# A graph network kernel on one core: GpSimd clears a scratch tile between gathers, and payload and row slots are handed over by single units

## What is computed

```python
# src, dst: (50000,) node numbers; dst is sorted
h = relu(layernorm(x))
x = x + mlp(h + segment_sum(relu(h[src] + edge_attr_16 @ We + be), dst))      # layer 0
h = relu(layernorm(x))
x = x + ten_steps_of_weighted_sums(h, edge_weight, src, dst)                   # layer 1
h = relu(layernorm(x))                                                         # layer 2, three sublayers:
hx = h @ W_node[l]; ef = relu(edge_attr_3 @ W_e1[l] + b_e1[l]) @ W_e2[l] + b_e2[l]
a = sigmoid(relu(concat(hx[dst], hx[src], edge_attr_3) @ Wa1[l] + ba1[l]) @ Wa2[l] + ba2[l])
h = maybe_relu(layernorm(segment_sum(a * (hx[src] + ef), dst) + bias[l])) + h
h = relu(layernorm(x))
x = x + segment_sum(silu(bn(concat(h[src], h[dst] - h[src]) @ W.T)), src)      # layer 3
```

## Time and profile before

| | |
|---|---|
| three timed runs | 4567.13, 4567.83, 4573.78 us |
| profiled execution, first to last instruction | 5635.3 us (its only time that is given) |
| busy in it: PE, DVE, ACT, POOL | 3433.8, 2812.2, 928.0, 3082.6 us |
| mean granted TensorE clock in it | 0.781 |
| gathers (L770) | 2080, 2085.0 us busy |

### The profile page before, as it was taken

The page is one execution under the profiler, slowest core; times in us unless marked ns, Lnnn a source line. Parts: engine busy times, 40 slices in busy tenths (PEclk is TensorE's granted clock), DMA queues, the critical chain, the costliest instruction groups (busy, mean ns, idle before and its releaser), DMA issues.

```text
span 5635.3 us, 80038 instructions
## 1 busy us (share of the span) xinstructions
PE 3433.8 (61%) x20001; PEld 2425.2 (43%) x20012; DVE 2812.2 (50%) x10008; ACT 928.0 (16%) x3266; POOL 3082.6 (55%) x3058
## 2 busy tenths in 40 slices
PE   2440078878889999656656556666566666344444
PEld 2330034444433444355556455555455556233333
DVE  7840088878621111355555455555555556533333
ACT  0000023333200000011112111112111112111111
POOL 3787676656688880145555345555255554355544
PEclk9999999989899999777777577777677777555555
DMA  4311123323599999411111211112111112011101
GB/s 139 82 26 9 47 67 74 83 70 80 133 331 344 356 352 356 165 40 43 42 43 42 38 41 43 42 43 41 38 43 43 42 43 40 18 20 19 19 18 21
DMA packets 293594, 498.20 MB, mean 88 GB/s; under 512 B 169174, under 2 KB 207203, under 8 KB 291962
## 3 DMA queue, kind: packets, MB, share of 16 engines
q1 hardware_dynamic: 118407, 339.94, 17.0%
q0 software_dynamic: 92160, 115.72, 11.2%
q10 hardware_dynamic: 82800, 40.01, 2.5%
HBM read 435.57 MB, written 58.97 MB: 88 GB/s over the span
## 4 chain that ended last, share of the span: by engine, by line
PE 38%; another core or an unknown queue 21%; DVE 14%; issue 13%; POOL 8%; ACT 2%; DMA 1%; DVEq 1%; ACTq 1%; SPq 0%; POOLq 0%
PE ps L1502 34%; POOL rows_dst L755 8%; DVE arena L1103 3%; DVE arena L1102 2%; PE ps L1728 2%; DVE arena L1121 1%; DVE arena L1119 1%; PE ps L1605 1%; DVE arena L1117 1%; DMA arena<-in_edge_attr_dram 1%; PE ps L1680 1%; DVE arena L1275 1%; ACT arena L1468 1%; DVE arena L1280 1%
## 5 line engine op out<-in xcount | busy, mean ns | idle before, releaser
L770 POOL DMA_INDIRECT arena<-table,arena x2080 | 2085.0, 1002 | 2200.4 <-DMA arena<-rows_dst 1299.9
L1502 PE MATMUL ps<-arena 128*128 128x96 f32 (+3 forms) x9176 | 1605.9, 354 | 573.3 <-issue 174.3
L1502 PEld LDWEIGHTS ps<-arena 128*128 128x128 f32 (+3 forms) x9176 | 1138.9, 207 | 953.3 <-issue 623.6
L1605 PE MATMUL ps<-ident,arena 128*96 128x128 f32 x416 | 149.9, 360 | 1123.1 <-ACT arena L1468 570.6
L1102 DVE TENSOR_SCALAR arena<-iota_row_b,arena 128x128 bf16<-128x128 bf16 x1664 | 438.3, 264 | 695.4 <-remote 518.6
L1502 PE MATMUL ps<-arena,nodes 125*64 125x500 f32 (+2 forms) x3144 | 649.6, 538 | 27.2 <-DVEq L1194 16.5
L755 POOL DMA_INDIRECT rows_dst<-stage,arena x400 | 483.7, 1209 | 196.3 <-issue 121.6
L1103 DVE TENSOR_SCALAR arena<-iota_row_b,arena 128x128 f32<-128x128 bf16 x2080 | 582.5, 298 | 0.0
L1605 PEld LDWEIGHTS ps<-ident,arena 128*96 128x96 f32 x416 | 65.3, 157 | 1190.5 <-ACT arena L1468 588.3
L1115 DVE TENSOR_TENSOR arena<-ps,arena 128x256 f32<-128x256 f32 x416 | 175.4, 422 | 787.3 <-remote 614.9
L728 POOL DMA_INDIRECT rows_src<-stage,stage_at x400 | 485.1, 1213 | 118.5 <-issue 116.6
(11 more groups left out here) (284 smaller groups left out, 3858.7 us busy)
## 6 DMA issues: line engine op xcount, KB each, us to landing
arena<-dense SPq DMA_DIRECT2D x240, 750.0 KB
nodes<-dense SPq DMA_DIRECT2D x60, 750.0 KB
dense<-arena ACTq DMA_DIRECT2D x150, 250.0 KB
arena<-table,arena POOLq DMA_INDIRECT x2080
arena<-dense SPq DMA_DIRECT2D x60, 500.0 KB
arena<-rows_dst SPq DMA_DIRECT2D x208, 96.0 KB
arena<-dense SPq DMA_DIRECT2D x6, 2000.0 KB
arena<-pair_rows SPq DMA_DIRECT2D x12, 976.6 KB
```

What stands on the lines that cost most here:

```text
L770: nc.gpsimd.indirect_dma_start(rows[:, u, k, 0:width], None, frm, bass.IndirectOffsetOnAxis(ap=p[:, c, j, c_other:c_other + 1].bitcast(I32 ...
L1502: return nc.tensor.matmul(to, lhsT, rhs, start=start, stop=stop, skip_group_check=True)
L1605: nc.tensor.transpose(to, pay[:, c, j:j + K, :].rearrange("p k c -> p (k c)"), ident[:]).then_inc(tr_ready, 1)
```

## The change

`CH` goes from 4 to 8, so `UC` is 1: every payload DMA carries one unit (48 KB instead of 96 KB for `pay`, 8 KB instead of 16 KB for `pay2`; 520 such DMAs instead of 260), and the waits for `pay_in` and `slots_free` stand ahead of four gathers instead of eight. TensorE and VectorE wait for `pay_in` at each unit instead of each second one. The carved arrays keep their total size. After each gather GpSimd waits until all scratch clears before this one are complete, and then clears `rest`, 100 float32 in each of 128 partitions; 2080 clears in all. `rest` is read by nobody.

```diff
-CH = 4
+CH = 8
 UC = U // CH
 CT = K * UC
...
+        rest = sb("rest", [128, 100])
...
+        rested = sem("rested")
...
                                     bass.IndirectOffsetOnAxis(ap=p[:, c, j, c_other:c_other + 1].bitcast(I32), axis=0)).then_inc(gathered[u], 16)
 
+                                hold(pool, rested, m * BODY + (u * K + k + 1))
+                                nc.gpsimd.memset(rest[:], 0.0).then_inc(rested, 1)
+
+            pool.sem_inc(rested, 1)
             pool.wait_ge(filled, 16 * 8)
             scatter_dst()
```

## The result

The changed kernel takes 4707.15 us (median of four runs), the kernel before 4567.68 us in the same session. The ratio is 1.0301, with a 95% interval of 1.0288 to 1.0313: slower by 3.0%, 139 us. Forecast were 4699 us and slower.

What follows compares the result with a forecast made beforehand. GpSimd's issue of gathers was taken to bound passes 1 to 4. The clears' 116 us there plus 15 us in pass 0 gave 131 us on 4567.83: 4699 us, 2.9% more, range 4575 to 4860 us.

Steps and rivals of the forecast that it cites:

- The stops belong to the profiled execution: Passes 1 to 4: GpSimd's idle gaps of 4.98 and 10.2 us occur only in the profiled execution, not timed runs.
- GpSimd's issue of gathers bounds passes 1 to 4: Passes 1 to 4, timed: GpSimd needs 5.00 us for a unit's four gathers, the compute side about 4.4.
- The clear, 0.07 us a gather, 116 us: Passes 1 to 4: a clear behind each of 1664 gathers adds 0.07 us, 116 us; ends 0 and 300 us.
- The first reading: Between two gathers: clear 0.18 us plus 0.18 us behind it, 0.36 us for 0.30, so 0.06 us more.
- The second reading: Between two gathers: a clear adds a third of what three copies added between two scatters, 0.11 us.
- the price of 200 us by the spacing of starts: Passes 1 to 4: clear costs its start spacing, some 0.12 us, with the full 0.30 us behind: 200 us.
- The wait costs 0: GpSimd's wait for the clear before, behind each gather: cost 0, covered by the running gather's 0.94 us.
- Pass 0, 15 us: Pass 0: VectorE 6.15 and GpSimd 5.93 us a unit nearly level; clears add 0.14 us a unit, 15 us.
- Single units, 0: Payload DMAs of one unit, 520 instead of 260: no wait removed in passes 1 to 4, cost 0.
- No change: Rival: the clear fits into a fixed 0.30 us between two indirect DMAs; 4568 us, chance 0.11.
- Heavier: Rival: clear and full 0.30 us follow each other, or clears collide with VectorE in pass 0; 4850 to 4920 us, chance 0.16.
- Faster: Rival: the ring of row slots bounds the timed run and single units free slots earlier; about 4500 us, chance 0.06.

Runs made afterwards that it cites:

- E1: The kernel before, run again with no edit: 4568.65 us, ratio 0.9994.
- E7: The kernel before with two of the four gathers of each unit left out, all else computed: 4191.43 us, ratio 0.9195 to the kernel before.
- E6: The changed kernel with a clear of 200 elements instead of 100: 4871.62 us, ratio 1.0688 to the kernel before.
- E10: The changed kernel with a clear of 60 elements instead of 100: 4634.31 us, ratio 1.0141 to the kernel before.
- E4: The changed kernel with a clear of 1 element instead of 100: 4604.51 us, ratio 1.0074 to the kernel before.
- E5: The changed kernel with the wait but no clear, GpSimd's queue raising the semaphore itself: 4567.84 us, ratio 1.0015 to the kernel before.
- E8: The changed kernel with two scratch tiles in turn, each clear waiting for the clear two before: 4678.98 us, ratio 1.0255 to the kernel before.
- E9: The changed kernel with waits and clears in pass 0 alone: 4571.01 us, ratio 1.0008 to the kernel before.
- E2: The changed kernel without the clears and their waits, CH = 8 kept: 4574.83 us, ratio 1.0009 to the kernel before.
- E3: The changed kernel with CH back at 4, so the clears alone: 4703.63 us, ratio 1.0295 to the kernel before.

## Why the prediction was right, point by point

- **The stops belong to the profiled execution.** Right; E1 shows the same kernel with a span of 4570.0 us. Expecting them again in the changed kernel's profile was wrong; it has none. The comparison of totals had put the unit of passes 1 to 4 between 4.72 and 5.13 us; it is 5.03 (1.258 x 4).
- **GpSimd's issue of gathers bounds passes 1 to 4.** Right (E7, and VectorE's wait on the gathers in E1). The compute side's time for a unit of pass 2 was read too high, 4.40 us where E7 has 3.98: the units between two stops did not show its free rate. It did not matter for the sum.
- **The clear, 0.07 us a gather, 116 us.** The first reading of the earlier trace rows, the end of the instruction between plus a fixed rest, was the right one: 0.20 + 0.16 = 0.36 us for 0.30, and E6 and E10 follow it. It alone gives 0.059 x 1660 = 98 us (a pass has 415 intervals). The second reading, a share for each instruction however short, is refuted by E4. So is the price of 200 us by the spacing of starts, a spacing with the full 0.30 us behind it. The changed kernel's trace has 0.16 us behind a clear where the earlier trace rows had 0.18 behind a copy, and 0.20 us for a clear where the two clears of the earlier trace rows gave 0.18.
- **The wait costs 0.** Wrong, in "its cover is the 0.94 us of the gather". A satisfied wait adds nothing to the passes (E5), but a wait for the latest clear leaves GpSimd's queue only about one gather of lead, and the queue's pause of 1.6 us in every 88 gathers then reaches the engine: 18 breaks of 1.5 us, 27 us. In E8, which gives back one gather of lead, passes 1 to 4 are 26 us shorter than in the changed kernel, and in E4 they are 29 us longer than in E1 with an unchanged interval.
- **Pass 0, 15 us.** Wrong; it is 0 (698.2 us after, 699.4 in E1; E9). I took VectorE's busy time, 6.15 us a unit, for the pace. The pace is 6.7 us (699.4 / 104). GpSimd's own need there, gathers, clears and gaps without its waits for payload, rises from 6.1 us a unit in E1 to 6.5 in the changed kernel and 6.7 in E6. It stays that low because the gathers get shorter as the clears come in: 1244 ns on average in E1, 1176 with clears of 100 elements, 1142 with 200. VectorE waits for no gather there in any of the three. E7 shows the pass indifferent to half of the gathers. The term failed by calling two rates nearly level without the pass's own pace.
- **Single units, 0.** Right as far as can be told, 0 to 8 us (E2, E3).
- **The sum.** Passes 1 to 4 grew from 522.4, 523.2, 521.9, 521.1 to 555.1, 557.3, 555.9, 554.3 us, 134 us together: 98 for the interval, 27 for the breaks, and the remaining 9 mostly for clears that last longer than the median (mean 209 ns in pass 1 against 200). The timed runs differ by 139 us; the last 5 aren't placed. Forecast were 131, with 116 for the interval, 0 for the wait and 15 for pass 0. That the total was closer than its parts is luck: the pause of the queue, which the forecast did not know, stood in for the 15 us of pass 0 and for a 0.07 that was 0.059.

The rivals fell as follows. *No change* is refuted by the ratio, though its mechanism, a fixed 0.30 us in which a clear fits, is real for a short enough clear (E4). *Heavier* is refuted by the interval of 1.31 us. *Faster* through the ring is refuted by E2.

**Open.** What the queue does in the 1.6 us every 88 gathers isn't shown; only that it comes with clears of 1 to 200 elements, without clears (E5), and with one more instruction a gather in the queue. Whether it is also there in the kernel before can't be read: that queue has too few records. Why the first profile of the kernel before had its stops isn't known either; they came in one execution and in none of the twelve other profiles.

## What to carry to other kernels

When a profiled execution is much longer than the timed runs, look for gaps that end for several engines at once, take them out, and compare the engines' rates without them: here the slowest of these rates named the bound. The cost came out within 8 us, in part by luck. An engine that only issues DMAs can bound a loop; what counts there is the interval from issue to issue, and a small instruction between two issues costs the time by which it and the gap behind it (0.16 us here) exceed the gap that stands there anyway (0.30 us). Don't let such a queue wait for its own engine's latest instruction: here a wait for the one two back gave it enough lead to hide its pauses, 26 us.

## What was not expected of the hardware

- Between two indirect DMAs GpSimd leaves 0.30 us, and the runs fit one rule: a clear leaves the interval as it is as long as its end plus 0.16 us lies inside, and lengthens it by the excess otherwise: clears of 1, 60, 100 and 200 elements lasted 0.12, 0.16, 0.20 and 0.28 us and gave intervals of 1.252, 1.275, 1.311 and 1.395 us.
- GpSimd's queue pauses by about 1.6 us once in 88 gathers (18 times in 1664). With a lead of eleven to twelve gathers the engine shows nothing of it (E5); in the changed kernel, where the wait keeps the queue about one gather ahead, the engine loses 1.5 us each time.
- Clears beside VectorE's work are stretched: 273 ns on average in pass 0 and 209 ns in pass 1, and single ones by 0.12 us (E6). In pass 0 VectorE is busy for 91% of the time, in pass 1 for 76%. The Trainium skill (SBUF — State Buffer, SBUF: two separate sides) describes an exclusive lock on the port pair that VectorE and GpSimd share, which could be the cause; the rows agree with it in direction, and no run here separates it from other causes.
